# Three fp16 passes in place of fp32 for the second routed feed forward's down product and both products of the last feed forward

## The reference

```
# sixth (L2_ffn): 16 experts of width 64, top 2, and a shared gated part of width 256
shared = (silu(x @ sfc1.T) * (x @ sfc2.T)) @ sfc3.T
h = silu(einsum('td,ehd->teh', x, w1))
moe = einsum('teh,te,edh->td', h, dispatch, w2)
x = x + moe + shared
# eighth (L3_ffn): ternary weights and a low rank term
h = bitlinear(x, w_fc) + gate * (x @ v.T @ fast_b.T @ u.T)
r = max(h, 0)
x = x + bitlinear(r * r, w_proj)
```

## Time and profile before

| | |
|---|---|
| median of 3 runs | 1506.32 us (1502.78 to 1506.56) |
| the profiled execution's own time | 1501.59 us |
| its span | 1499.6 us |
| mean granted TensorE clock | 0.956 |
| PE, PEld busy | 1380.4 us (92%), 852.6 us (57%) |
| DVE, ACT, POOL busy | 1020.2 us (68%), 887.5 us (59%), 810.0 us (54%) |
| second routed feed forward | about 1150 to 1262 us of the span |
| attention before the last sublayer | about 1262 to 1465 us |
| last feed forward | about 1465 to 1499.6 us |

### The profile page before, as it was taken

The page is one execution under the profiler, slowest core; times in us unless marked ns, Lnnn a source line. Parts: engine busy times, 40 slices in busy tenths (PEclk is TensorE's granted clock), DMA queues, the critical chain, the costliest instruction groups (busy, mean ns, idle before and its releaser), DMA issues.

```text
span 1499.6 us, 36708 instructions
## 1 busy us (share of the span) xinstructions
PE 1380.4 (92%) x14354; PEld 852.6 (57%) x14354; DVE 1020.2 (68%) x2498; ACT 887.5 (59%) x1470; POOL 810.0 (54%) x764
## 2 busy tenths in 40 slices
PE   5999999997879999999978999887997998999998
PEld 3566666665657777777733444333575565445445
DVE  5877777788744434443758988875787366677764
ACT  4677777774759999999834444422234232555542
POOL 5677877776659899989854343212452002335310
PEclk9999999999989999999979999998979799899999
DMA  9000000000013110001001110000000000000000
GB/s 276 2 9 9 9 9 9 2 2 22 23 33 98 61 45 14 28 28 50 30 5 32 65 33 33 29 20 10 1 3 10 0 1 4 5 9 5 6 1 29
DMA packets 26083, 39.59 MB, mean 26 GB/s; under 512 B 7060, under 2 KB 13113, under 8 KB 25433
## 3 DMA queue, kind: packets, MB, share of 16 engines
q1 hardware_dynamic: 25368, 35.58, 7.3%
q0 software_dynamic: 576, 2.10, 0.7%
HBM read 38.72 MB, written 1.05 MB: 27 GB/s over the span
## 4 chain that ended last, share of the span: by engine, by line
PE 70%; DVE 19%; issue 6%; ACT 4%; POOL 2%; DMA 0%; SPq 0%; POOLq 0%; DVEq 0%; ACTq 0%
PE bank L1702 10%; PE bank L1643 10%; PE bank L698 5%; DVE sbuf L837 4%; PE bank L1140 4%; PE bank L636 4%; PE bank L2168 3%; PE bank L652 2%; PE bank L1209 2%; PE bank L1926 2%; PE bank L1160 2%; PE bank L1190 2%; PE bank L2147 2%; PE bank L1232 2%; DVE sbuf L854 2%
## 5 line engine op out<-in xcount | busy, mean ns | idle before, releaser
L1653 ACT ACTIVATE sbuf<-bank,sbuf 128x512 f32<-128x512 f32 (+1 forms) x512 | 322.8, 684 | 28.4 <-PE bank L1643 16.4
L1673 POOL TENSOR_TENSOR sbuf<-sbuf 128x512 f16<-128x512 f32 x256 | 304.6, 1198 | 54.8 <-ACT sbuf L1653 53.6
L313 POOL TENSOR_TENSOR sbuf<-sbuf 128x2 f32<-128x2 f32 (+1 forms) x48 | 39.6, 825 | 357.6 <-DVE sbuf L308 357.6
L1702 PEld LDWEIGHTS bank<-sbuf 128*128 128x128 f16 x3072 | 193.8, 98 | 66.7 <-issue 7.2
L1702 PE MATMUL bank<-sbuf 128*128 128x128 f16 x3072 | 214.2, 220 | 6.3 <-DVEq L1790 6.3
L1643 PE MATMUL bank<-sbuf 128*128 128x512 f16 x768 | 207.9, 380 | 0.0
L837 DVE TENSOR_REDUCE sbuf<-bank 128x4 f32<-128x1024 f32 x128 | 156.4, 1222 | 65.0 <-PE bank L652 52.6
L1103 POOL TENSOR_TENSOR sbuf<-sbuf 128x512 f16<-128x512 f32 x128 | 148.0, 1176 | 71.5 <-ACT sbuf L1319 70.9
L1785 DVE SCALAR_TENSOR_TENSOR sbuf<-bank,sbuf 128x128 f32<-128x128 f32 x256 | 71.8, 342 | 164.2 <-PE bank L1702 163.9
L698 PE MATMUL bank<-sbuf 128*32 128x256 f32 x2048 | 137.2, 386 | 1.6 <-ACT sbuf L785 1.6
L785 ACT ACTIVATE sbuf<-sbuf 128x1024 f32<-128x1024 f32 x64 | 67.6, 1057 | 97.4 <-DVE sbuf L854 95.9
(11 more groups left out here) (284 smaller groups left out, 2743.8 us busy)
## 6 DMA issues: line engine op xcount, KB each, us to landing
sbuf<-w SPq DMA_DIRECT2D x32, 256.0 KB, 2.9
sbuf<-bias_t SPq DMA_DIRECT2D x4, 1024.0 KB, 13.7
sbuf<-ctx_t SPq DMA_DIRECT2D x24, 128.0 KB, 3.6
sbuf<-bias_q POOLq DMA_DIRECT2D x4, 512.0 KB, 11.4
sbuf<-mask_t SPq DMA_DIRECT2D x8, 256.0 KB, 2.7
sbuf<-bias_t SPq DMA_DIRECT2D x8, 256.0 KB, 3.1
sbuf<-mask_q SPq DMA_DIRECT2D x8, 256.0 KB, 3.5
sbuf<-bias_q SPq DMA_DIRECT2D x8, 256.0 KB, 4.0
```

Source lines behind the costliest of these rows:

```text
L1653: last = act.activation(to, bank[u % 4][:, :], ACT.Gelu, bias=b1[u // U][:, u % FT0:u % FT0 + 1], scale=1 / SCALE)
L1673: g.tensor_tensor(hid16[1][:, u % BUFS, :], hid[:, u % 4, :], hid16[0][:, u % BUFS, :], ALU.subtract)\
L1702: last = pe.matmul(bank[4 + out_no % 2][:, j * P:(j + 1) * P], hid16[h][:, u % BUFS, j * P:(j + 1) * P], w2_16[p][:, w, f * D:(f + 1) * D] ...
```

## The change

Both products of the last feed forward and the down product of the second routed one become three fp16 passes. Weights are scaled by 256 and split once; the sum is scaled back in the add. For each unit ACT makes the upper fp16 half of `hid` and POOL subtracts for the lower. LAG grows to 4 in both stages. POOL's `weights` in the retention also converts `wd`. POOL makes fp16 halves of x for the last feed forward during the attention. The square of the last sublayer is formed on DVE from the PSUM bank and the relu, and on ACT as `Square`. The add of the second routed feed forward moves from unit 3 to unit 5 of the next chunk, the scale from 4 to 7, the turn from 7 to 9. The retention's context is loaded in two pieces, not four, and five small constant loads share one semaphore with two others. The core of the diff:

```diff
@@ first sublayer and far loads
-                sp.dma_start(tile[0:src.shape[0]], src).then_inc(near_in, 16)
+                sp.dma_start(tile[0:src.shape[0]], src).then_inc(const_in, 16)
...
-                v.wait_ge(const_in, 32)
+                v.wait_ge(const_in, 16 * (2 + len(near)))
...
@@ narrow_attention, pool
-                    if gated and b >= 3:
+                    if b >= 3:
                         lead.halves(g, b - 3)
-                if gated:
-                    lead.halves(g, B - 3)
+                lead.halves(g, B - 3)
...
@@ gated_feed_forward
-            LAG = 2
-            RING, HIDS = 4, 6
+            LAG = 4
+            RING, HIDS = 4, 8
...
-            TURN_AT = 7
+            TURN_AT = 9
...
-                for w, to, n in ((wg, wg16, NT), (wu, wu16, shared)):
+                for w, to, n in ((wg, wg16, NT), (wu, wu16, shared), (wd, wd16, NT)):
...
                 def down(m):
-                    pe.wait_ge(s["hidden"], m + 1)
+                    pe.wait_ge(s["low"], m + 1)
...
-                        last = pe.matmul(bank[DOWNS[c % 2]][:, j * P:(j + 1) * P], hid[:, m % HIDS, j * P:(j + 1) * P],
-                                         wd[:, t, :], start=first and j == 0, stop=last_, skip_group_check=True)
+                        for k, (h, w) in enumerate(PASSES):
+                            last = pe.matmul(bank[DOWNS[c % 2]][:, j * P:(j + 1) * P],
+                                             hid16[h][:, m % HIDS, j * P:(j + 1) * P], wd16[:, w, t * D:(t + 1) * D],
+                                             start=first and j == k == 0, stop=last_ and k == 2, skip_group_check=True)
...
+                def high_hidden(m):
+                    act.wait_ge(s["hidden"], m + 1)
+                    wait(act, s["down"], m - HIDS + 1)
+                    act.activation(hid16[0][:, m % HIDS, :], hid[:, m % RING, :], ACT.Copy).then_inc(s["high"], 1)
...
+                    if m:
+                        high_hidden(m - 1)
...
-                    wait(v, s["down"], m - HIDS + 1)
+                    wait(v, s["low"], m - RING + 1)
...
-                    if m >= NT and m % NT == LAG + 2:
+                    if m >= NT and m % NT == LAG + 3:
                         k = m // NT - 1
                         after.scale(v, 2 * k, 2 * k + 2)
...
             def pool(g):
-                for k in range(CHUNKS):
-                    after.power(g, 2 * k, 2 * k + 2)
+                for m in range(len(units)):
+                    if m == at_unit(0, 5):
+                        halves(g, B - 1)
+                    g.wait_ge(s["high"], m + 1)
+                    g.tensor_tensor(hid16[1][:, m % HIDS, :], hid[:, m % RING, :], hid16[0][:, m % HIDS, :], ALU.subtract)\
+                     .then_inc(s["low"], 1)
+                    if m >= NT and m % NT == LAG + 1:
+                        k = m // NT - 1
+                        after.power(g, 2 * k, 2 * k + 2)
+                after.power(g, B - 2, B)
...
@@ last_feed_forward
-            NT, LAG, RING = 4, 2, 4
+            NT, LAG, RING, HIDS = 4, 4, 4, 8
...
                 if m == 26:
-                    v.scalar_tensor_tensor(fc_t, fast, far["gate"][:, 0:1], second[:, :], ALU.mult, ALU.add)\
+                    c.step(v.scalar_tensor_tensor(fast, fast, far["gate"][:, 0:1], second[:, :], ALU.mult, ALU.add)).settle()
+                    c.step(v.tensor_scalar(fc16[:, 0, :], fast, SCALE, None, ALU.mult)).settle()
+                    v.scalar_tensor_tensor(fc16[:, 1, :], fast, SCALE, fc16[:, 0, :], ALU.mult, ALU.subtract)\
                      .then_inc(s["made"], 1)
...
-                    v.tensor_copy(proj_t, second[:, :].rearrange("p (t d) -> p t d", d=D)).then_inc(s["made"], 1)
+                    c.step(v.tensor_scalar(proj16[:, 0, :], second[:, :], SCALE, None, ALU.mult)).settle()
+                    v.scalar_tensor_tensor(proj16[:, 1, :], second[:, :], SCALE, proj16[:, 0, :], ALU.mult, ALU.subtract)\
+                     .then_inc(s["made"], 1)
...
-                    act.activation(acted[:, m % RING, :], bank[INNER[m % 2]][:, :], ACT.Relu).then_inc(s["acted"], 1)
+                    act.activation(acted[:, m % RING, :], bank[INNER[m % 2]][:, :], ACT.Relu, scale=1 / SCALE)\
+                       .then_inc(s["acted"], 1)
+                    act.wait_ge(s["acted"], m + 1)
+                    wait(act, s["down"], m - HIDS + 1)
+                    act.activation(hid16[0][:, m % HIDS, :], acted[:, m % RING, :], ACT.Square).then_inc(s["high"], 1)
...
+            def pool(g):
+                for m in range(len(units)):
+                    if m == TURN_AT + 1:
+                        for k in (B - 2, B - 1):
+                            halves(g, k)
...
@@ retention
-            LOADS = 4
+            LOADS = 2
...
-                for b in (B - 2, B - 1):
-                    lead.halves(g, b)
+                lead.halves(g, B - 2)
```

More of the change, by code:

```diff
@@ L497, in ready, with narrow_attention @@
                 eng.wait_ge(g_t, self.base["turned"] + k + 1)
-        def narrow_attention(layer, nm, late, ahead, after, lead=None):
-            gated = lead is not None
+        def narrow_attention(layer, nm, late, ahead, after, lead):
+            gated = layer == 1
             masked = layer == 1
@@ L2067, in gated_feed_forward @@
                 "gated",
+                "high",
+                "low",
             )}
@@ L2084, in gated_feed_forward @@
             gates16 = take([B * S], F16)
-            assert top[0] <= 35072
+            wd16 = take([2, NT * D], F16)
+            assert top[0] <= 36800
             top[0] = body
             acted = take([RING, CHUNK])
-            hid = take([HIDS, CHUNK])
-            assert top[0] <= 17728
+            hid = take([RING, CHUNK])
+            hid16 = [take([HIDS, CHUNK], F16) for _ in range(2)]
+            assert top[0] <= 20800
             HIGH, LOW, ROWS = slice(0, E), slice(32, 32 + E), 64
@@ L2221, in scalar @@
                         after.copy(act, 2 * c, 2 * c + 2, bank[UPS[0]])
+                high_hidden(len(units) - 1)
             def vector(v):
@@ L2245, in add @@
                     xs = x[:, k * CT:(k + 1) * CT, :]
[L2246 to L2247 removed]
+                    v.scalar_tensor_tensor(xs, bank[DOWNS[k % 2]][:, :].rearrange("p (t d) -> p t d", d=D), 1 / SCALE, xs,
+                                           ALU.mult, ALU.add).then_inc(x_done, 1)
                     v.wait_ge(x_done, x0 + k + 1)
@@ L2295, in gated_feed_forward @@
             return FeedLead(gate, weights, halves, append_programs)
+        EndLead = namedtuple("EndLead", "halves programs")
         def last_feed_forward(nm, tail):
-            s = {k: sem("f3_" + k) for k in ("inner", "acted", "hidden", "down", "made", "made_pe", "stored")}
+            s = {k: sem("f3_" + k) for k in ("inner", "acted", "hidden", "high", "low", "down", "x16", "made", "made_pe", "stored")}
             x0 = x_steps[0] + B
-            NT, LAG, RING = 4, 2, 4
+            NT, LAG, RING, HIDS = 4, 4, 4, 8
+            SCALE = 2.0 ** 8
+            PASSES = ((0, 0), (0, 1), (1, 0))
             units = [(c, t) for c in range(CHUNKS) for t in range(NT)]
-            top[0] = 35072
-            fc_t = take([F0])
-            proj_t = take([4, D])
-            assert top[0] <= 36800
-            top[0] = 17728
+            top[0] = 28864
+            fc16 = take([2, F0], F16)
+            proj16 = take([2, F0], F16)
+            assert top[0] <= 29888
+            x16 = take([2, B * S], F16)
+            top[0] = 20800
             fc_e = take([4, D])
@@ L2317, in last_feed_forward @@
             acted = take([RING, CHUNK])
+            top[0] = body
             hid = take([RING, CHUNK])
-            assert top[0] <= 29888
+            hid16 = [take([HIDS, CHUNK], F16) for _ in range(2)]
             INNER, DOWNS, TURNED = (0, 1), (6, 7), 2
@@ L2397, in inner @@
                     if t == 0:
-                        pe.wait_ge(nrm_xt, nm.ready(2 * c + 1))
+                        pe.wait_ge(s["x16"], 4 * c + 4)
                     if m >= 2:
                         pe.wait_ge(s["hidden"], m - 1)
-                    pe.matmul(bank[INNER[m % 2]][:, :], fc_t[:, t * P:(t + 1) * P], xn_t[:, c * CHUNK:(c + 1) * CHUNK],
-                              start=True, stop=True).then_inc(s["inner"], 1)
+                    for k, (w, xk) in enumerate(PASSES):
+                        last = pe.matmul(bank[INNER[m % 2]][:, :], fc16[:, w, t * P:(t + 1) * P],
+                                         x16[:, xk, c * CHUNK:(c + 1) * CHUNK], start=k == 0, stop=k == 2)
+                    last.then_inc(s["inner"], 1)
                 def down(m):
                     c, t = units[m]
-                    pe.wait_ge(s["hidden"], m + 1)
+                    pe.wait_ge(s["low"], m + 1)
                     if t == 0:
@@ L2411, in down @@
                     for j in range(CT):
```

(10 more changed lines are left out.)

43 lines of the change are left out of this document (25 added, 18 removed).

## The result

The changed kernel takes 1509.4 us (median of 20 runs, 1503.5 to 1513.3) against 1505.5 for the kernel before (20 runs, 1495.7 to 1509.8). The ratio is 1.0034, with a 95% interval of 1.0023 to 1.0046: it is slower by about as much as a measurement of this kernel can tell. The forecast was 1509.8. The profiled execution has a span of 1501.6 us, against 1499.6. The kernel before ran again beside each group of experiments, with medians of 1504.5, 1504.7 and 1503.8, so medians from different groups can differ by 1 to 2 us for that alone. One run of all, in experiment 6, took 2538 us and is left out of that kernel's ratio.

The account below looks back on a forecast made before the run. PE was taken to set the second routed feed forward, ACT and POOL nearly free. Terms 5.3 + 3.4 - 13.9 + 13 - 4.5 = +3.3, plus 0.2, on the median 1506.3 gave 1509.8 us, range 1497 to 1521.

Parts of the forecast that it names:

- The retention, +8.7 forecast: Retention: third matrix's conversion at the head of POOL's queue delays PE's mix, +5.3 us, with +3.4 for the clock.
- The clock's part: Retention: after PE stands still 4.8 us, 7 us run at half clock, +3.4 us, ends 0 and +7.
- PE in the second routed feed forward, -13.9: Second routed feed forward: cheaper fp16 down passes save PE 12.0 us, plus 1.9 for units at half clock.
- The 12.0 at full clock: Second routed feed forward: down saves 0.32 us for each of 32 routed units and 0.22 for 8 shared ones.
- The 1.9 for units at half clock: Second routed feed forward: some six units run at half clock and save twice as much, 1.9 us more.
- DVE's delays, +13: Second routed feed forward: hidden comes late behind DVE's blocks and PE waits; parts sum to 15.2, taken as +13 us.
- The stage as a whole: Second routed feed forward: PE's gain of -13.9 us and DVE's delays of +13 nearly cancel.
- The last feed forward, -4.5: Last feed forward: POOL's subtractions set its end, last down at 1491.4 instead of 1496.0, -4.5 us, bounds -7 and -2.
- Square's table load, set at nothing: Last feed forward, ACT: alternating relu and Square costs no table load; one load of 1.3 us as upper end.
- Absorbed delays: Rival, second routed feed forward: DVE's idle time absorbs delays, stalls 4 instead of 13, clock loss 0; 1497 us, chance 0.22.
- The clock falls at unit 28 to 31 and each scale waits for POOL: Rival, second routed feed forward: PE gap near 2.7 us drops the clock, +3.4, scale operations +6; 1519 us, chance 0.28.
- POOL slower than its row: Rival, last feed forward: subtraction takes 1.38 us, not 1.16, and passes PE's 1.32, costing 3.5; 1513 us, chance 0.05.

Follow-up runs that it names:

- experiment 6, narrow: Changed kernel with POOL's subtraction in the second routed feed forward on 32 of 512 columns: 1501.1 us, ratio to the kernel before 0.9957.
- after: The changed kernel itself, first profiled execution: median 1509.4 us, ratio to the kernel before 1.0034.
- after_again: The changed kernel once more, unchanged, for a second profiled execution: second routed feed forward 115.0 us against 109.4.
- before_wd, experiment 2: Kernel before, plus three POOL operations the size of the third matrix's conversion in the retention, results unread: 1510.3 us, ratio 1.0034.
- no_last, experiment 4: Changed kernel with the last feed forward's tables and products in fp32 as before: 1515.3 us, ratio to the kernel before 1.0077.
- sched: Changed kernel with DVE's table work for the last feed forward placed where DVE idles: 1507.2 us, ratio to the kernel before 1.0007.
- before: The kernel before the change, first profiled execution: median 1505.5 us.
- before_again: The kernel before once more, unchanged, for a second profiled execution: second routed feed forward 107.0 us against 111.4.
- no_gated, experiment 3: Changed kernel with the second routed feed forward as before, no third conversion, last halves back in the retention: 1499.5 us, ratio to the kernel before 0.9961.
- experiment 1, wd_late: Changed kernel with the third matrix's conversion behind the retention's powers instead of ahead: 1502.8 us, ratio to the kernel before 0.9989.
- experiments 5 and 7: Changed kernel, DVE's table work moved to idle places: 1507.2 us; also third conversion behind the powers: 1499.0; also norm's transposes in another bank: 1494.8.
- experiment 8: Changed kernel with late third conversion, spread table work, transposes in another bank, and five more DVE moves: 1494.7 us, ratio to the kernel before 0.9937.

## Why the prediction was right

The total was right, 1509.8 forecast and 1509.4 measured, and that it came so close is in part luck. By the medians the change costs 3.9, by the two profiled executions 1.9, and the sum said 3.3. Of the sum's three parts two were too pessimistic (the retention, the last feed forward) and one too optimistic (the second routed feed forward), and the errors nearly cancel.

**The retention, +8.7 forecast (5.3 and 3.4 for the clock).** Right in mechanism, step by step: the conversion adds 6.46 (6.5 forecast), DVE waits, PE waits 4.96 (4.8). The trace puts PE's release at the add behind the mask (L2744), 0.3 us later than the mask that the forecast named. The stage took 66.0 us on the mean of six profiles with the conversion at the head (`after`, `after_again`, `before_wd`, `no_last`, `sched`, `narrow`) and 58.7 on the mean of three without it (`before`, `before_again`, `no_gated`): 7.3. In the pair of profiles of before and after the 6.9 us are 4.4 of idle time and 2.5 of longer busy time. By medians it is 5.8 (experiment 2) and 8.6 (experiment 1: 6.6, and the 2 that the moved conversion still costs). The term was 0 to 3 too large. The clock's part came out near its size for a reason that the forecast didn't have. It took one stretch of 7 us behind the wait; the trace has two of 3 to 4 us, one behind the wait and one at the last mix, behind a busy PE. Its row for it was misread too: in the kernel before the clock was at 0.50 already ahead of the wait of 3.31, from 1156.4 to 1158.2, behind one of 2.91.

**PE in the second routed feed forward, -13.9.** The 12.0 at full clock stands: the quiet unit steps 1.74 (1.73 forecast). The 1.9 for units at half clock doesn't. That counted stretches at half clock as a place where the new form saves double, as if there would be as many as in one profile of before. The mean granted clock of the stage was 0.90 in four executions with the fp32 product (0.88, 0.92, 0.89, 0.89) and 0.89 in the four with the fp16 product and DVE's queue as changed (0.91, 0.87, 0.91, 0.86), so no such gain shows.

**DVE's delays, +13.** Measured: 13.5 us of waits less 2.2 that were there, +11.3. By place, forecast and measured:

| place | forecast | measured |
|---|---|---|
| units 11 and 12, behind `choose` | +2.5 | 0.89 + 2.15 = 3.0 |
| behind add, `low`, scale, ternary of 15 to 19 | +4 | 1.40 + 2.12 = 3.5 |
| units 28 to 31, with ACT's copy (the 0.8 was for units 20 and 30) | 5.8 + 0.8 | 0.54 + 1.36 + 1.10 + 1.27 - 0.72 = 3.6 |
| units 34 to 37 | +1.1 | 0.48 + 0.54 - 1.05 = 0 |
| end of the stage | +1.0 | 0.93 + 0.27 = 1.2 |

The method, counting DVE's work over a few units against 1.73 us each, found every place, and its sum (15.2, cut to 13 for overlap) was high mostly in units 28 to 31. Four scale operations took 2.55, 1.10 and 1.96, where 2.3 was forecast. What I hadn't priced is the port's hold on very short operations: the first two of `choose`, 0.19 and 0.17 us in the kernel before, took 1.17 and 1.18.

**The stage as a whole** was forecast at -0.9. The mean of four profiles with the fp16 product (109.4, 115.0, 110.2, 113.7) is 112.1 us, of four with the fp32 product (111.4, 107.0, 110.8, 110.7) 110.0: +2.1, with a scatter of 4 to 6 us inside each group. By medians three comparisons bear on it. With the last feed forward new in both kernels, `wd_late` is 3.3 above `no_gated`, and 2.0 of that is what the moved conversion still costs: +1.3. With it old in both, `no_last` is 5.0 above `before_wd`. What is left of the whole is 3.9 - 6.6 (retention, experiment 1) + 5.9 (last feed forward, experiment 4) = +3.2, or +1.2 with the 2.0 taken to the retention. So the step that failed is this term: it gained nothing and cost 1 to 5 us.

Where it failed shows in the same eight profiles. PE's idle time in the stage rose from 8.5 to 19.3 us on the mean, as forecast (+10.8). Its busy time fell from 101.5 to 92.7, by 8.8 and not by 13.9. In `after` and `wd_late` (clock 0.91) it is 89.6 and 90.3, so the passes gave their 12 us there. In `after_again` and `no_last` (0.87 and 0.86) it is 95.5 and 95.6, and half of the gain is gone to stretches at half clock. How often the one and the other come, four executions can't say.

**The last feed forward, -4.5.** Right in mechanism (POOL sets its end), too small in size. The fp16 form takes 25.1 to 26.3 us in nine profiles; the fp32 form takes 30.6, 32.3, 32.3 and 32.4 in four. The step took the earlier trace rows, where the stage ran nearly all at full clock, and 30.6 was the best of the four. When more of the stage is at half clock, both forms pay: 1.7 us for the fp32 form (clock 0.89 instead of 0.94) and 0.8 to 1.1 for the fp16 form, which POOL sets (0.87 instead of 0.94). By medians the gain is 5.9 (experiment 4) or 4.9 (experiment 3). POOL itself was a little faster than forecast, 20.6 us from first to last subtraction instead of 21.5.

**Square's table load, set at nothing.** No row of a table load stands in the last feed forward, so setting it at nothing was right. The section of the Trainium skill that the forecast cites ("ScalarE: Activation LUTs", Table sets) says which functions are in every set and not which other sets hold Square, so the load of 1.3 us didn't follow from it.

**The rivals.** *Absorbed delays* fell: 11.3 us of waits stand there. *The clock falls at unit 28 to 31 and each scale waits for POOL* fell as a mechanism. Those waits are 0.54 to 1.36, and the passes behind them took 0.81 or 0.82. Nor do single waits of 2.1 decide it: behind 2.15 and 2.12 the passes took 1.46 and 1.44 in the first execution of the changed kernel and 0.82 and 0.81 in the next, as in `wd_late` and `no_last`. *POOL slower than its row* fell: 1.12 us.

## What to carry to other kernels

When a change adds work to a function that an engine runs early, look up what is queued behind it there: here three operations that hold up a tiny power cost 6 us, and moving them behind it is a small edit. When the bound engine gets faster, what was slack for the engine in step with it is gone: count that engine's work over each few units against the new step, and spread blocks to the units where it idles, which gave 2 to 4 us in experiments 5 and 7 and nothing more in experiment 8. For a stage that can run at two clocks, take its duration from several executions before reading 2 us out of it; PE's waits repeat from one to the next, the stage's time doesn't.

## What was not expected of the hardware

- A DVE operation of 0.19 us took 1.17 beside POOL's subtractions and 0.25 without them, and one of 0.17 took 1.18 and 0.16. The loss doesn't shrink with the operation: what counts is whether one of POOL's is under way when it starts.
- The same code, with the same waits to a few hundredths, ran this stage in 109.4 and in 115.0 us, at a granted clock of 0.91 and of 0.87. What starts a stretch at half clock behind a wait near 2 us is left open. Behind the waits of 3.3 at the gate (1.46 us for three passes in both executions of both kernels; each follows a wait of 2.9 by less than 2 us of work) and of 4.9 to 5.9 in the retention it came each time.
- A delay early in the retention was followed by a second stretch at half clock some 37 us later, in six profiles of six, in the one shown behind 12 us of PE without a pause. None of the seven without the delay has it.
